# Packing 25 buckets of edges into 19 dense tiles in the edge network of a four-layer graph kernel

## The reference

```
x = layernorm(x + L0(x))    # two rounds of x@W, sum over edges, + b
x = layernorm(x + L1(x))    # edge network, below
x = layernorm(x + L2(x))    # message layer
x = layernorm(x + L3(x))    # polynomial of the graph operator, 10 rounds
```

```
edge_in = concatenate([h[row], h[col], dist])              # 129
e   = silu(silu(edge_in @ eW1 + eb1) @ eW2 + eb2)          # 128
agg = segment_sum(e, row)
out = silu(concatenate([h, agg]) @ nW1 + nb1) @ nW2 + nb2
```

## Time and profile before

| | |
|---|---|
| time, median of 3 runs | 1791.71 us (1789.79 to 1793.77) |
| time of the profiled execution | 1792.04 us |
| its span | 1790.6 us, mean granted TensorE clock 0.939 of full speed |
| TensorE busy | 1543.8 us (86%), 16702 matmuls |
| VectorE, ScalarE, GpSimd busy | 1184.2, 538.4, 43.7 us |
| stages (us from the start) | placement to 197, tables to 216, counts to 372, L0 to 508, edge network to 1080, L2 to 1172, L3 to the end |

### The profile page before, as it was taken

One profiled execution on the slowest core, in us unless ns is written; L12 is line 12 of the kernel. 1 busy time (PEld: TensorE's weight loads), 2 busy tenths in 40 slices (PEclk: granted clock), 3 DMA queues, 4 the chain that ended last, 5 costly groups with the idle time before them and its releaser, 6 DMA issues. The chain is left out here.

```text
span 1790.6 us, 45172 instructions
## 1 busy us (share of the span) xinstructions
PE 1543.8 (86%) x16702; PEld 1424.3 (80%) x16702; DVE 1184.2 (66%) x3535; ACT 538.4 (30%) x1011; POOL 43.7 (2%) x59
## 2 busy tenths in 40 slices
PE   0645479969969999999999996959999999999993
PEld 0434367769958888888888884959999999999993
DVE  5999768844365555555555545757867677677775
ACT  0299689921024444444444441010000000000000
POOL 1100100000000000000000003000000000000000
PEclk9878699979989999999999997969999999999997
DMA  1000044420024333333222206000000000000000
GB/s 21 6 0 0 20 132 140 140 73 2 2 86 136 117 111 111 111 111 111 76 79 92 91 4 159 2 5 2 2 3 2 3 2 2 3 2 3 2 2 20
DMA packets 35102, 88.86 MB, mean 50 GB/s; under 512 B 21031, under 2 KB 22047, under 8 KB 34953
## 3 DMA queue, kind: packets, MB, share of 16 engines
q1 hardware_dynamic: 30321, 79.38, 14.7%
q10 hardware_dynamic: 4410, 7.43, 1.8%
q0 software_dynamic: 224, 0.13, 0.0%
HBM read 65.68 MB, written 21.18 MB: 49 GB/s over the span
## 5 line engine op out<-in xcount | busy, mean ns | idle before, releaser
L1605 PE MATMUL L_psA<-L_parts,mat 125*128 125x192 bf16 x6250 | 517.2, 246 | 0.0
L1605 PEld LDWEIGHTS L_psA<-L_parts,mat 125*128 125x128 bf16 x6250 | 515.5, 98 | 1.1 <-DVE L_parts L1683 1.0
L1243 DVE TENSOR_TENSOR L_e<-L_ps_z,L_eb 128x512 f32<-128x512 f32 (+1 forms) x101 | 66.4, 657 | 139.7 <-PE L_ps_z L1087 138.3
L1076 PEld LDWEIGHTS L_ps_pre<-L_drow,mat 128*128 128x128 bf16 (+1 forms) x1950 | 125.0, 98 | 36.8 <-issue 1.1
L1670 DVE TENSOR_REDUCE L_sumr<-L_psA 125x64 f32<-125x192 f32 x250 | 89.3, 357 | 77.7 <-PE L_psA L1605 76.6
L1076 PE MATMUL L_ps_pre<-L_drow,mat 128*128 128x128 bf16 x1950 | 139.1, 220 | 0.0
L1070 PE MATMUL L_ps_pre<-mat,L_pp 125*128 125x512 bf16 (+1 forms) x525 | 135.6, 367 | 2.5 <-DVE L_pp L1209 2.5
L574 DVE TENSOR_TENSOR onehot<-iota_bf,codes 128x1024 bf16<-128x1024 bf16 (+1 forms) x175 | 106.0, 648 | 31.0 <-PE ps_extra L636 23.6
L1547 ACT COPY L_wk<-L_Wk 128x64 f32 (+1 forms) x10 | 2.0, 242 | 402.7 <-PE L_psA L1605 402.6
L1243 DVE TENSOR_TENSOR mat<-L_ps_z,L_eb 128x512 f32<-128x512 f32 x74 | 48.0, 649 | 102.3 <-PE L_ps_z L1087 101.0
L685 PE MATMUL L_psA<-L_gparts,mat 125*128 125x192 bf16 x1250 | 109.1, 248 | 4.5 <-DVE L_gparts L698 4.5
(11 more groups left out here) (267 smaller groups left out, 2496.8 us busy)
## 6 DMA issues: line engine op xcount, KB each, us to landing
mat<-rows_d SPq DMA_DIRECT2D x25, 832.0 KB, 4.3
L_drow<-rows_d SPq DMA_DIRECT2D x25, 728.0 KB
m_d<-panel SPq DMA_DIRECT2D x25, 684.2 KB
mat<-m_d SPq DMA_DIRECT2D x16, 684.2 KB
mat<-m_d ACTq DMA_DIRECT2D x9, 684.2 KB
L_drow<-rows_d SPq DMA_DIRECT2D x25, 84.5 KB
m_d<-panel SPq DMA_DIRECT2D x25, 79.4 KB
mat<-m_d SPq DMA_DIRECT2D x16, 79.4 KB
```

Of the source, the lines that this page charges most:

```text
L1076: last = nc.tensor.matmul(ps_pre[bank][:, i * P:(i + 1) * P], w, drow[k][:, cc * P:(cc + 1) * P], start=False, stop=(r == 2 and cc == tile ...
L1243: nc.vector.tensor_tensor(grp(e2_of(k, g)), grp(ps_z2[bank]), eb2[:].unsqueeze(1).broadcast_to([P, len(tiles), H]), ALU.add).then_inc(bias ...
L1605: last = nc.tensor.matmul(ps[:, 0:3 * D], t.mat[0:B, kb, b * B:b * B + P], parts[src][:, kb].rearrange("p r d -> p (r d)"), start=(kb == 0 ...
```

## The change

The source block's 25 first tiles are no longer one for each bucket. Bucket number k of a source block may begin anywhere in the 128 slots from 96 k (`STEP`) on. Its offset there is what its predecessors overflowed: offset of the next = max(offset + bucket's total - 96, 0). The block's own bucket keeps at most 108 edges (`DIAG`) beyond its offset; the others go to the rest tile as before. 24 steps of 96 and one window of 128 are 2432 slots, 19 tiles of 128; with the rest tile there are 20 (`ST`), 5 groups of 4.

- `place_edges`: 18 new matmuls of ones against `two` give all bucket totals; VectorE makes `chain` from them, scans it (`tensor_tensor_scan`) into `off`, casts it to bf16 (`off_bf`), and one more matmul for each window adds the offset to the ranks. Before the first rank is finished TensorE waits for the offsets. The slot arithmetic behind the ranks is longer: the bucket's window is turned by a multiple of 32 so that a slot's partition is its place in the dense tile.
- `edge_tables`: VectorE assembles the dense tile table `t.dense` from pieces of the buckets' source field (8 copies, 4 adds), before the other tables. Source rows are stored from it; the four other fields are still stored bucket by bucket, turned back, by pieces: 41 DMAs in place of 6.
- `count_matrices`: the one-hots of the last two tiles have a buffer of their own, `last_hot`. No instruction is added.
- `edge_network`: 5 groups. `layer1` multiplies by `srow` of 20 tiles, and by each bucket's `drow` in its window (`windows_of`); a window that crosses a group's border is two pieces. `layer2`, `by_src`, the silus, biases and one-hots run over 20 tiles. `keep_agg` and `node1` stand at group 3, `node2` at 4, `product_p` at 3, `split_p` at 4, the row comparisons at 2 and 3. `xs` moves into `room`, and small buffers of L2 and L3 move into `src1` and `dense`.

```diff
+STEP = 96
+DIAG = 108
+ST = 20
...
+                for h, (lo, hi) in enumerate(wins):
+                    dve.wait_ge(totals, h + 1)
+                    D1(nc.vector.tensor_scalar(
+                        chain[:, :, 1 + lo:1 + hi].rearrange("p c b -> p b c"),
+                        ps_slot[h][:, 0:(hi - lo) * NC].rearrange("p (b c) -> p b c", c=NC)[:, :, 0:NB], -float(STEP),
+                        None, ALU.add))
+                D1.wait()
...
+                D1(nc.vector.tensor_scalar(own, own, float(DIAG - STEP), None, ALU.min))
+                D1.wait()
+                D1(nc.vector.tensor_tensor_scan(offs, steps, zero[:], 0.0, ALU.add, ALU.max))
+                D1.wait()
+                nc.vector.tensor_copy(off_bf[:, :, 0:NB], off[:, :, 0:NB].rearrange("p c b -> p b c")
+                                      ).then_inc(chained, 1)
...
-                D1(nc.vector.scalar_tensor_tensor(tmp[:], rank[:], float(CAP), diag[:], ALU.is_gt, ALU.mult))
+                D1.wait()
+                each = lambda ap: ap.unsqueeze(2).broadcast_to([P, NB, W])
+                D1(nc.vector.tensor_tensor(slot[:], rank[:], each(over_at[:]), ALU.subtract))
+                D1.wait()
+                D1(nc.vector.scalar_tensor_tensor(tmp[:], slot[:], 0.0, diag[:], ALU.is_gt, ALU.mult))
                 D1(nc.vector.tensor_scalar(col[:], sblk[:], -1.0, float(NB), ALU.mult, ALU.add))
                 D1.wait()
-                nc.vector.scalar_tensor_tensor(slot[:], tmp[:], -float(CAP), rank[:], ALU.mult, ALU.add
-                                               ).then_inc(slotted, 1)
+                D1(nc.vector.tensor_tensor(slot[:], tmp[:], each(over_at[:]), ALU.mult))
+                D1(nc.vector.scalar_tensor_tensor(diag[:], tmp[:], 0.0, each(turn[:, 0:NB]), ALU.is_equal, ALU.mult))
+                D1.wait()
+                D1(nc.vector.tensor_tensor(rank[:], rank[:], slot[:], ALU.subtract))
+                D1.wait()
+                D1(nc.vector.tensor_tensor(slot[:], rank[:], diag[:], ALU.add))
+                D1(nc.vector.tensor_scalar(valid[:], rank[:], 1.0, None, ALU.is_ge))
+                D1.wait()
+                D1(nc.vector.tensor_scalar(diag[:], slot[:], float(P), -float(P), ALU.is_gt, ALU.mult))
+                D1(nc.vector.scalar_tensor_tensor(valid[:], rank[:], float(CAP), valid[:], ALU.is_le, ALU.mult))
+                D1.wait()
+                D1(nc.vector.tensor_tensor(slot[:], slot[:], diag[:], ALU.add))
+                D1.wait()
+                nc.vector.tensor_tensor(slot[:], slot[:], valid[:], ALU.mult).then_inc(slotted, 1)
...
+                pe.wait_ge(keyed, NB // SET)
+                twos = two[:].rearrange("p (b g) c -> p b g c", g=W // 2)
+                for h, (lo, hi) in enumerate(wins):
+                    for g in range(W // 2):
+                        last = nc.tensor.matmul(
+                            ps_slot[h][:, 0:(hi - lo) * NC].rearrange("p (b c) -> p b c", c=NC), c.ones_bf[:],
+                            twos[:, lo:hi, g, :], start=(g == 0), stop=(g == W // 2 - 1))
+                    last.then_inc(totals, 1)
...
+                    if b == 0:
+                        pe.wait_ge(chained, 1)
+                    nc.tensor.matmul(ps[:, 0:W * NC].rearrange("p (j c) -> p j c", c=NC), share[:],
+                                     off_bf[:, b, :].unsqueeze(1).broadcast_to([P, W, NC]), start=False, stop=True
+                                     ).then_inc(ranked, 1)
...
+                v.tensor_copy(tile[:, :, third(0)], src[:, 0:NB, every(0)])
+                for rows, to, of in (((0, 64), 1, 1), ((64, 96), 1, 1), ((96, P), 1, 2),
+                                     ((0, 32), 2, 2), ((32, 64), 2, 2), ((64, P), 2, 3)):
+                    p = slice(*rows)
+                    v.tensor_copy(tile[p, :, third(to)], src[p, 0:NB, every(of)])
+                v.tensor_copy(tile[:, :, ST - 1], src[:, NB, :]).then_inc(packed, 1)
...
+                    last = v.tensor_tensor(tile[p, :, to], tile[p, :, to], src[p, 0:NB, every(of)], ALU.add)
+                last.then_inc(packed, 1)
...
+                sp.wait_ge(row_out, 1)
+                for u in range(5):
+                    sp.dma_start(main[u, 0:ST, 0:5], row_sb[u * ST:(u + 1) * ST, 0:5, :]).then_inc(rows_out, 16)
                 sp.wait_ge(row_out, 4)
                 for u in range(5):
-                    sp.dma_start(main[u, 0:NB], row_sb[u * NB:(u + 1) * NB, 0:NB, :]).then_inc(rows_out, 16)
-                sp.dma_start(blocks[:, NB, :], row_sb[:, NB, :]).then_inc(rows_out, 16)
-                sp.wait_ge(rows_out, 16 * 6)
+                    for m in range(4):
+                        some = slice(u * NB + m, (u + 1) * NB, 4)
+                        r = STEP * m % P
+                        sp.dma_start(main[u, m:NB:4, 5:NB, 0:P - r], row_sb[some, 5:NB, r:P]).then_inc(rows_out, 16)
+                        if r:
+                            sp.dma_start(main[u, m:NB:4, 5:NB, P - r:P], row_sb[some, 5:NB, 0:r]
+                                         ).then_inc(rows_out, 16)
+                sp.dma_start(blocks[NB:5 * NB, NB, :], row_sb[NB:5 * NB, NB, :]).then_inc(rows_out, 16)
+                sp.wait_ge(rows_out, 16 * 41)
...
+    def windows_of(g):
+
+        for cc in range(NB):
+            lo, hi = max(STEP * cc, 4 * P * g), min(STEP * cc + P, 4 * P * (g + 1), (ST - 1) * P)
+            if lo < hi:
+                yield cc, cc * P + lo - STEP * cc, lo - 4 * P * g, hi - lo
+        if g == len(EG) - 1:
+            yield NB, NB * P, 3 * P, P
...
-                        if was and g == 4:
-                            node1(*was)
-                        if was and g == 5:
+                        if was and g == 3:
+                            node1(*was)
+                        if was and g == 4:
                             node2(*was)
...
-                        if g == 4:
+                        if g == 3:
                             product_p(b + 1, 1 - k)
```

More of the change, by code:

```diff
@@ L87, in place_edges @@
         iotac = sb("iotac", [P, NC, DUP], BF16)
-        upto = sb("upto", [P, P], BF16)
+        upto, share = sb("upto", [P, P], BF16), sb("share", [P, P], BF16)
+        turn = sb("turn", [P, 28], F32)
+        chain, off = sb("chain", [P, NB, NC], F32), sb("off", [P, NB, NC], F32)
+        zero = sb("zero", [P, NB * NC], F32)
+        off_bf = sb("off_bf", [P, NB, NC], BF16)
+        over_at = sb("over_at", [P, NB], F32)
         ps_cnt = s.enter_context(nc.psum_tensor("ps_cnt", [P, 512], F32))
@@ L900, in edge_network @@
         wd3 = sb("wd3", [P, 3, H], BF16)
-        o += 2 * HOT
+        o += 2 * DENSE
+        xs = [room[:, o + i * 2 * B:o + (i + 1) * 2 * B].bitcast(F32) for i in range(2)]
+        o += 4 * B
         rest = room[:, o:o + 8 * H].bitcast(F32)
@@ L1071, in layer1 @@
                                          start=(r == 0), stop=False)
-                    for i, cc in enumerate(tiles):
+                    for cc, of, to, n in pieces:
                         for r in range(3):
@@ L1490, in polynomial_layer @@
         safe, scale2 = sb("safe", [B, NB], F32), sb("scale2", [B, NB], F32)
-        sumr, diff, rest = ([sb(f"{n}{i}", [B, D], F32) for i in range(2)] for n in ("sumr", "diff", "rest"))
+        sumr = [sb(f"sumr{i}", [B, D], F32) for i in range(2)]
+        spare = t.dense[0:B].rearrange("p b t -> p (b t)").bitcast(F32)
+        diff = [sb("diff0", [B, D], F32), spare[:, 0:D]]
+        rest = [spare[:, D:2 * D], spare[:, 2 * D:3 * D]]
         old = lambda lo, hi: t.src1[0:B, lo * NB:hi * NB].rearrange("p (b s) -> p b s", s=hi - lo)
@@ L2132, in program @@
         t.src1 = sb("src1", [P, NT], F32)
+        t.dense = sb("dense", [P, NB, ST], BF16)
         t.wsum = sb("wsum", [B, NB, WP], F32)
```

158 lines of the change are left out of this document (87 added, 71 removed).

## The result

The changed kernel takes 1738.90 us, the median of 4 runs (1734.33 to 1743.08), against 1791.88 before (4 runs, 1789.79 to 1793.77). The ratio is 0.9704, 95% interval 0.9677 to 0.9732: 3% faster. Forecast was 1724, range 1709 to 1747. The sign and the range held, the middle was 15 us too low. The profiled execution took 1737.73 us, its span 1735.7, against 1790.6: 54.9 us of span to account for.

A forecast was written before the change was run, and what follows sets the result against it. The prediction took TensorE's columns to bound the edge network's loop. Edge network -87, placement +3.5 and +4, tables +11.5 sum to -68 us from the profiled 1792.04, giving 1724 us, range 1709 to 1747.

The forecast's parts named there:

- The edge network: Edge network's loop: fewer TensorE columns cut the block period from 21.45 to 17.9 us, -87 us in all.
- The split windows: Destination matmuls of the edge network: 78 become 90 a block, taken as +0.2 us a block.
- The bound of -91: Edge network's cheaper bound: a gain of 91 us if splitting windows costs nothing.
- Rival 2: Edge network: split matmuls cost by number, 0.056 us or more each, +12 us, 1736; chance 0.09.
- Rival 1: Edge network: TensorE stalls at keep_agg or split_p, 0.5 to 1 us a block, 1736 to 1749; chance 0.11.
- The tables: Tables stage: packing on VectorE and 41 DMAs issued 0.5 us apart, +11.5 us (5 to 16.5).
- rival 3: Tables: row stores cost 1.95 us each, 1784; kernel slower from 2.16 us per DMA on; chance 0.03.
- The placement: Placement: offset chain before the first rank, +3.5 us, and longer slot arithmetic, +4; together +7.5.
- Counts and L0: Count stage and L0: same instructions with buffers moved, 0 us.
- Rivals 3 and 4: The fourth: placement overflows a window's 128 slots, so the general program runs, at no known price; chance 0.01.
- The three stages give back more than 27: Stages before the edge network: forecast wrong if they give back more than 27 us or less than 10.
- The loop's mark: Edge network's loop: forecast wrong if its gain is not about 87 us.

The follow-up runs named there:

- experiment 4: Edge network of the changed kernel behind the placement and tables of the kernel before, dense table filled with zeros; 1705.93 us, ratio 0.9514.
- experiment 5: Changed kernel with no destination window crossing a group's border, 78 matmuls a block rather than 90, right places left out; 1732.48 us, ratio 0.9667.
- experiment 6: Changed kernel with all 25 dense windows cut into 32 and 96 columns, 153 matmuls a block, right places left out; 1756.60 us, ratio 0.9792.
- experiment 7: Changed kernel with product_p at the end of group 4 rather than group 3 on TensorE; 1782.30 us, ratio 0.9938.
- experiment 10: Changed kernel without turning, each tile place's field store cut into four of all 25 rows and 5 of 20 runs; 1716.2 us, one run.
- experiment 12: Changed kernel with the four other fields' stores first, on two queues, dense stores last, field rows in bucket order; 1717.13 us, ratio 0.9576.
- experiment 1: Changed kernel with the four other fields stored bucket by bucket, not turned back, 5 DMAs in place of 35; 1715.71 us, ratio 0.9574.

## Why the prediction held, and where it did not

- **The edge network, -87 forecast, -89.5 in the trace and -86.6 in time by experiment 4.** Right, and for the reason given: TensorE's columns are the price. Layer 1's wide matmuls, layer2 and by_src kept their times and come 5 times in place of 6.5. The period is 17.90. The split windows cost 0.22 us a block (taken: 0.2). The bound of -91 without split cost was added up wrongly: 25 x 3.73 less 1 is 92.
- **Rival 2, a price by the number of matmuls**, is refuted: 12 ns and not 56 for each extra one (experiments 5 and 6).
- **Rival 1, a hand-over stall**, is refuted in the changed kernel by the absence of any idle time in the loop; experiment 7 shows that the place I named was the right one to watch. ScalarE copies `aggs` at 701.94 to 702.19 and node1 starts at 702.92, without a wait:

```profile
701.94 0.25 ACT L1259 COPY L_aggs<-L_ps_agg 128x125 f32<-128x125 f32 x1
```

- **The tables, +11.5 forecast, +23.6 measured.** This is the step that failed. "Small DMAs issue at 0.34 to 0.64 apart. I take 0.5" was the mis-sized term: 35 of the 41 cost 0.80. I took all small DMAs for one kind and the middle of the earlier trace rows. The three rows there were loads into whole neighbouring rows; the new stores pick every fourth one. My upper bound for the term, +16.5, was below the truth as well, though rival 3 named the term: its own bound of 1.95 stood in the same rows, and the truth lies between them. A second error of 2.0 us came from pricing VectorE's pieces by one row of 0.21 us, where the packing takes 0.31 to 0.44 each. A piece of 32 to 64 rows and 150 elements isn't the piece of that row. So the total lies in the range by luck as well: the range had room for a dearer split and for rival 1, which did not come, and the tables' excess went into that room.
- **The placement, +7.5 forecast, +8.6 measured.** Right in its parts. The second copy out of PSUM, scan and cast, 0.7 us longer together, and the ranks, of which 0.6 us came back where 1.1 was taken, make the difference.
- **Scatter +1.5, where 0 was forecast.** Not the change. In the fourteen profiles of this study the scatter takes either 103.8 to 103.9 us (ten, that of before among them) or 105.4 (four: the changed kernel, experiments 4, 10 and 12), and experiment 4 has the scatter of the kernel before. The difference is the last 18 matmuls, beside which no other work is left: 1.8 us at a granted clock of 1.00 in the ten, 3.3 at 0.50 in the four. TensorE's rows and the windows over them, first before, then the changed kernel:

```profile
194.92 1.77 PE L366 MATMUL ps_slot<-rows,ohr 128*128 128x208 bf16 x18 [2.28 <-DVE rows L350]
...
194.90:196.70 1.80, 1.77 (x18) 1.54 (x18) 0.00 (x0) 0.14 (x1) 0.00 (x0) 1.00 0.00 0
```

```profile
203.53 3.28 PE L420 MATMUL ps_slot<-rows,ohr 128*128 128x208 bf16 x18 [1.49 <-issue]
...
203.50:206.80 3.30, 3.27 (x18) 2.49 (x18) 0.00 (x0) 0.16 (x1) 0.00 (x0) 0.50 0.00 0
```

The mean clock of the stage does not tell this: it is 0.83 before and 0.79 in the changed kernel, but experiment 5 has 0.79 too, and 103.8 us:

```profile
101.50:205.30 103.80, 57.06 (x450) 46.86 (x450) 97.76 (x125) 100.75 (x275) 0.00 (x0) 0.79 0.00 0
```

- **Counts and L0 +1.8, where 0 was forecast.** They range from 309.8 (experiment 1) to 314.4 us (changed) for the same instructions; the new placement ends at 101.5 to 104.1, and what follows the last `aggs` ranges from 717.2 to 723.1. Between two executions such stages differ by 1.5 to 6 us that no row of one trace shows. What makes them differ was not followed.
- **Rivals 3 and 4** did not come: 0.80 is far below the 2.16 us from which the stores would have made the kernel slower, and the fast program ran.
- "The three stages give back more than 27" was a mark by which I would be wrong, and it was passed (+33.7 with the scatter). The loop's mark was met.

## What to carry to other kernels

Where a stage ends in a barrier, count its DMAs and price each by a row of the same shape: direction, rows, and the stride between them. Without such a row take the dearest small DMA in the trace as the upper bound, not the middle one. When the issuing engine turns out to be the limit, look first for a second idle queue, then for stores that are ready earlier, and then for a row order that makes each store's rows neighbours; here the three took 13.7, 4.1 and 3.2 us off the stage. Cutting matmuls of 128 columns at a border is nearly free in a dense stream (12 ns each), while a whole group of tiles less is worth its columns.
